# A three-stage attention front in which queries go through transposed key weights, with two banks for outputs and values and a layer norm that is split between engines

## The reference, cut to what matters

```python
# parts 0 and 2 (weights Wq 256x256, Wk and Wv 128x256, Wo 256x256)
Q = query @ Wq + bq;  K = key @ Wk + bk;  V = key @ Wv + bv
weights = softmax(Q @ K.T * 256 ** -0.5, axis=-1)
return query + (weights @ V) @ Wo + bo
# part 1: softmax over the QUERY axis, and a layer norm at the end
q = emb @ Wq + bq;  k = latent @ Wk + bk;  v = latent @ Wv + bv
w = softmax(q @ k.T / 16, axis=1)
x = w @ v + emb
return (x - mean(x)) * rsqrt(var(x) + EPS) * gamma + beta
```

## Time and profile before

| | |
|---|---|
| median of 3 runs | 2909.15 us (2907.28 to 2910.56) |
| the profiled execution, its own time | 2909.43 us |
| its span in the trace | 2907.6 us (1.83 us lie around it) |
| busy share: PE, DVE, ACT, POOL | 96%, 59%, 45%, 40% |
| the front in the span | 0 to 215.77 us |
| granted TensorE clock over the span | 0.995 |

### The profile page before, as it was taken

How to read it: one execution, slowest core, us unless ns; L and a number is a source line. 1 busy time by engine, 2 the same in 40 slices (tenths; PEclk the granted TensorE clock), 3 DMA queues, 4 the chain that set the end, 5 groups by cost and what they waited for, 6 DMA issues and landing times.

```text
span 2907.6 us, 65193 instructions
## 1 busy us (share of the span) xinstructions
PE 2792.9 (96%) x24616; PEld 2324.0 (80%) x24616; DVE 1725.4 (59%) x6432; ACT 1304.0 (45%) x4273; POOL 1173.6 (40%) x1461
## 2 busy tenths in 40 slices
PE   6878999999999999999999999999999999999999
PEld 4656888888887888888888887888888888888887
DVE  3444665665665665665665665665665655665655
ACT  2223544544544544544544544544544544544444
POOL 2213454444444444444434444434444433333333
PEclk9999999999999999999999999999999999999999
DMA  6206334335334335343335343344353344232230
GB/s 207 102 3 203 90 132 152 93 108 182 102 138 136 103 113 168 111 144 117 113 121 151 120 152 104 115 133 145 119 159 94 118 133 127 93 116 80 95 111 18
DMA packets 178766, 350.36 MB, mean 120 GB/s; under 512 B 17997, under 2 KB 142486, under 8 KB 169110
## 3 DMA queue, kind: packets, MB, share of 16 engines
q1 hardware_dynamic: 168086, 195.18, 23.3%
q0 software_dynamic: 10368, 151.00, 14.2%
HBM read 307.48 MB, written 38.67 MB: 119 GB/s over the span
## 4 chain that ended last, share of the span: by engine, by line
PE 81%; DVE 8%; POOL 6%; issue 3%; ACT 1%; DMA 0%; SPq 0%; DVEq 0%; POOLq 0%; ACTq 0%
PE proj L680 19%; PE sum L1006 16%; PE score L680 14%; PE proj L700 7%; PE sum L680 6%; PE sum L700 4%; PE proj L1027 3%; PE sum L883 3%; PE score L859 2%; POOL rstd L583 2%; PE proj L964 2%; PE tr L964 1%; PE tr L870 1%; POOL stage_parts L551 1%; PE tr L1006 1%
## 5 line engine op out<-in xcount | busy, mean ns | idle before, releaser
L634 POOL TENSOR_TENSOR prob<-prob,rtotal 128x375 f32<-128x375 f32 x672 | 543.5, 811 | 607.6 <-DVE rtotal L1622 606.5
L1081 ACT ACTIVATE prob<-prob,negmax 128x375 f32<-128x375 f32 (+1 forms) x686 | 418.0, 609 | 438.8 <-DVE negmax L1613 406.9
L1006 PE MATMUL sum<-pT,ctx 32*128 32x224 f32 (+1 forms) x4608 | 500.6, 358 | 14.9 <-DVE qcT L1605 14.9
L1006 PE MATMUL tr<-pT,ctx 32*128 32x224 f32 (+1 forms) x4608 | 500.6, 358 | 0.0
L1006 PEld LDWEIGHTS sum<-pT,ctx 32*128 32x128 f32 (+1 forms) x4608 | 417.9, 185 | 68.1 <-issue 62.6
L1613 DVE CUSTOM_DVE_ANT_0 prob<-score,cbias 128x375 f32<-128x375 f32 x672 | 356.9, 531 | 183.3 <-PE score L680 179.5
L1006 PEld LDWEIGHTS tr<-pT,ctx 32*128 32x128 f32 (+1 forms) x4608 | 417.0, 185 | 0.0
L1631 DVE STREAM_TRANSPOSE pT<-prob 128x384 f32<-128x384 f32 x672 | 372.8, 558 | 0.0
L680 PE MATMUL score<-ctx_parts,qc_high 128*128 128x376 f32 x1344 | 368.3, 355 | 0.0
L590 POOL TENSOR_TENSOR prob<-prob,rtotal 112x448 f32<-112x448 f32 x200 | 186.0, 930 | 435.0 <-DVE rtotal L1483 435.0
L1160 ACT ACTIVATE prob<-prob,negmax 112x112 f32<-112x112 f32 x800 | 298.9, 376 | 90.6 <-DVE negmax L1501 90.6
(11 more groups left out here) (243 smaller groups left out, 5315.1 us busy)
## 6 DMA issues: line engine op xcount, KB each, us to landing
w_vq_parts<-sa_v_parts POOLq DMA_DIRECT2D x24, 2048.0 KB, 8.3
w_kf_parts<-sa_k_parts POOLq DMA_DIRECT2D x24, 2048.0 KB, 8.5
w_vq_parts<-sa_q_parts POOLq DMA_DIRECT2D x24, 2048.0 KB, 9.0
w_kf<-ff_w SPq DMA_DIRECT2D x48, 1024.0 KB, 7.0
ctx<-ctx SPq DMA_DIRECT2D x192, 176.0 KB
stage<-sa_kv SPq DMA_DIRECT2D x24, 512.0 KB, 3.8
sa_v_parts<-stage_parts SPq DMA_DIRECT2D x12, 1024.0 KB, 5.2
sa_q_parts<-stage_parts SPq DMA_DIRECT2D x12, 1024.0 KB, 4.7
```

What stands on the lines that cost most here:

```text
L634: pool.tensor_tensor(row, row, rtotal[:, G * SG + i:G * SG + i + 1].broadcast_to([P, S2]), ALU.mult).then_inc(prob_ready, 1)
L1006: ins = pe.matmul(bank[:, 0:HT * R], ctx4[keys_of, m // (HALVES // NB), j, :], pT[keys_of, m % 2, :, j * R:(j + 1) * R], start=j == 0, sto ...
L1081: act.activation(o, i, ACT.Exp, bias=negmax[0:rows, col:col + 1], scale=scale, accum_out=total[0:rows, col:col + 1]).then_inc(exp_ready, 1)
```

## The change

The change touches the front only. The score Q K^T = (q Wq + bq)(c Wk + bk)^T is computed in another order: the key weights are transposed once per part (`fwkT`, two transposes through `sum1`, copied by DVE), and `front_keyed(u)` multiplies the projected query by them (2 matmuls of 224 columns into `tr0`), which gives `fqk[u]`. The scores are then products of `fqk[u]` with the raw context `ctxT`. The key bias becomes a number per query, `fbk`: in parts 0 and 2 four matmuls with a single moving column per unit, added in `front_maxima`; in part 1 two matmuls of 224 columns, and a matmul with one row of ones ahead of each score matmul. The loop is shifted so that the scores of unit u follow the keyed queries of unit u + 1. Outputs go in turn to `sum1` and `proj1` (`FRONT_OUT`), values in turn to (`proj0`, `proj1`) and (`tr0`, `tr1`) (`FRONT_VALUES`). In the layer norm DVE only does (x - mean) * rstd; gamma and beta are applied by ACT on the transposed copy (`gain`, two new loads of 128 x 2 single elements) and by POOL on the residual (a multiplication, then `add_bias`, with beta added to the bias row once). Loads are grouped anew, so that PE starts without the context and the values' weights, and the identity matrix is made first on POOL.

```diff
@@ sync
+            for n, name in enumerate(("gamma", "beta")):
+                sp.dma_start(gain[:, n, :], front[1][name].rearrange("(k p) -> p k", p=P),
+                             allow_slow_non_contiguous=True).then_inc(rows_loaded, 16)
...
@@ gpsimd
             pool.wait_ge(rows_loaded, 16 * ROW_DMAS)
+            at = Place(FRONT_LOOP)
+            pool.tensor_tensor(fbias[0:S, 1, :], fbias[0:S, 1, :], fbias[0:S, 4, :], ALU.add).then_inc(pool_step, 1)
...
             for u in range(NU):
                 inverse_std(at, 1, u)
             for u in range(NU):
-                name = FRONT_TR[u % 2]
-                before = {"proj0": 9 * NU - NU, "sum0": 2 * NU + NU}[name]
-                pool.wait_ge(ready[name], at.at(name, before + u // 2 + 1))
+                pool.wait_ge(tn_ready, at.at("tn", u + 1))
+                pool.tensor_tensor(ftw[u][:, :, :], ftn[u][:, :, :], fbias[0:S, 3, :].unsqueeze(1).broadcast_to([S, NB, E]),
+                                   ALU.mult).then_inc(pool_step, 1)
+                pool.wait_ge(pool_step, at.at("pool", at.next("pool") + 1))
                 add_bias(fbias[0:S, 1, :], ftw[u])
@@ tensor
-            pe.wait_ge(setup_done, 1)
+            pe.wait_ge(ident_ready, 1)
...
+                def front_keyed(u):
+                    for e in range(EK):
+                        pe.wait_ge(taken[f"proj{e}"], at.emptied(f"proj{e}", queried[u, e]))
...
+                    bank = fill(at, "tr0")
+                    for e in range(EK):
+                        ins = pe.matmul(bank[:, 0:T2], fwkT[:, e, :], fqT[u][:, e, :], start=e == 0, stop=e == EK - 1)
+                    if n == 1:
+                        for e in range(EK):
+                            ins = pe.matmul(bank[0:1, T2:2 * T2], fcol[:, n, 1, e:e + 1], fqT[u][:, e, :],
...
+                    else:
+                        for b in range(NB):
+                            for e in range(EK):
+                                ins = pe.matmul(bank[0:S, T2 + b:T2 + b + 1], fqT[u][:, e, b * S:(b + 1) * S],
+                                                fcol[:, n, 1, e:e + 1], start=e == 0, stop=e == EK - 1)
...
                         if n != 1:
-                            project(at, name, [fqT[u][:, e, b * S:(b + 1) * S] for e in range(EK)],
-                                    [fkT[u][:, b, e, :] for e in range(EK)])
+                            ins = pe.matmul(bank[0:S, 0:S2], query, ctxT[:, ds(first, S2)], start=True, stop=True)
...
                 front_query(0)
-                front_keys(0)
                 for u in range(NU):
                     if u + 1 < NU:
                         front_query(u + 1)
-                    front_scores(u)
-                    if u + 1 < NU:
-                        front_keys(u + 1)
+                    front_keyed(u)
+                    if u > 0:
+                        front_scores(u - 1)
+                front_scores(NU - 1)
...
@@ vector
                 def front_normalise(u):
                     wait_rstd(at)
                     for b in range(NB):
-                        ins = dve.scalar_tensor_tensor(ftn[u][:, b, :], ftw[u][:, b, :], mv2[:, u, b, 0:1], fbias[0:S, 3, :],
-                                                       ALU.subtract, ALU.mult)
-                    link(at, ins)
-                    for b in range(NB):
-                        ins = dve.scalar_tensor_tensor(ftw[u][:, b, :], ftn[u][:, b, :], rstd2[:, u, b:b + 1], fbias[0:S, 4, :],
-                                                       ALU.mult, ALU.add)
+                        ins = normalise(ftn[u][:, b, :], ftw[u], b, u)
                     ins.then_inc(tn_ready, 1)
```

More of the change, by code:

```diff
@@ L304, in attention_layers @@
         front_loaded = [sem(f"front_loaded{n}") for n in range(3)]
+        front_q_loaded = [sem(f"front_q_loaded{n}") for n in range(3)]
+        ctxT_loaded = sem("ctxT_loaded")
+        ident_ready = sem("ident_ready")
         rows_loaded = sem("rows_loaded")
@@ L464, in _ @@
             load_first(stage[:, :, :], "sa_k", "first_w_k")
-            sp.wait_ge(taken["proj1"], Place(START).emptied("proj1", 0))
+            for name in FRONT_OUT:
+                sp.wait_ge(taken[name], Place(START).emptied(name, 0))
             load_w_o(0)
@@ L1089, in front_query, with front_keyed @@
                     plus(fqT[u][:, 0, :], bank[:, 0:T2], fcol[:, n, 0, 0:1]).then_inc(taken["proj0"], 1)
-                def front_keys(u):
-                    for b in range(NB):
-                        bank = filled(at, "proj0")
-                        plus(fkT[u][:, b, 0, :], bank[:, 0:S2], fcol[:, n, 1, 0:1]).then_inc(taken["proj0"], 1)
+                def front_keyed(u):
+                    bank = filled(at, "tr0")
+                    ins = copy(fqk[u], bank[:, 0:T2])
+                    if n == 1:
+                        ins = copy(fbk[u], bank[0:1, T2:2 * T2])
+                    else:
+                        ins = copy(fbk_col[u], bank[0:S, T2:T2 + NB])
+                    ins.then_inc(taken["tr0"], 1)
                 def front_softmax(u):
@@ L1115, in _ @@
                     bank = filled(at, name)
-                    copy(ftnT[u][:, :, :].rearrange("p k t -> p (k t)"), bank[:, 0:EK * T2]).then_inc(taken[name], 1)
+                    if n != 2:
+                        copy(ftnT[u][:, :, :].rearrange("p k t -> p (k t)"), bank[:, 0:EK * T2]).then_inc(taken[name], 1)
+                    else:
+                        for k in range(EK):
+                            ins = act.activation(ftnT[u][:, k, :], bank[:, k * T2:(k + 1) * T2], ACT.Identity,
+                                                 scale=gain[:, 0, k:k + 1], bias=gain[:, 1, k:k + 1])
+                        ins.then_inc(taken[name], 1)
+                if n == 1:
+                    act.wait_ge(rows_loaded, 16 * ROW_DMAS)
+                act.wait_ge(front_q_loaded[n], 16 * FRONT_Q_DMAS)
                 front_query(0)
-                front_keys(0)
                 for u in range(NU):
@@ L1453, in _ @@
                     front_normalise(NU - 1)
-            dve.wait_ge(taken["proj1"], Place(START).emptied("proj1", 0))
+            for name in FRONT_OUT:
+                dve.wait_ge(taken[name], Place(START).emptied(name, 0))
             def parts_of_normed(at, full, high, low):
```

176 lines of the change are left out of this document (105 added, 71 removed).

## The result

The changed kernel took 2872.33 us (median of 4 runs, 2871.38 to 2873.49) against 2909.0 us for the kernel before in the same session: a ratio of 0.9873, with a 95% interval of 0.9861 to 0.9884. It is 1.3% faster, where 1.5% and 2864 us had been forecast, and it lies just above the forecast's range of 2857 to 2872 us. Three executions among the runs of the experiments were slow ones (3458, 8118 and 6934 us) and are left out of all figures. The profiled execution took 2873.49 us with a span of 2871.6 us. START begins at 179.02 us, not at 215.77 and not at the 170.8 of the forecast. That START is 8.2 us late is what the forecast missed. Behind START everything moved with it: from there to the end of the span it is 2691.8 us before and 2692.6 us after.

The account below looks back on a forecast made before the run. PE bounds most of the span, with POOL's sixth round the limit before part 2. Savings 28.5 + 12.3 - 0.7 + 1.6 + 3.3 = 45.0 from 2907.6 give 2862.6; plus 1.83 less 0.28, 2864 us; range 2857 to 2872.

Parts of the forecast that it names:

- the forecast's 7, 14 and 5: PE starts 7 us earlier; part 0's score stage shrinks by 14 us, its outputs and values by 5.
- The term of 1.0 us for the two loads of single elements: Two added loads ahead of POOL's first round delay the rounds by 1.0 us (bounds 0 and 6.4).
- 12 of 112 columns at 5.56/24 = 0.23 (2.8): Part 1's score stage: twelve 112-column matmuls a unit at 0.23 us, 2.8 of the unit's 6.0 us.
- the margin of 11 us over POOL's rounds: End of part 1: PE's last output at 106 us, POOL answers from 114.7, a margin of about 11 us.
- The first sign of being wrong: Layer norm after part 1: the forecast is wrong if POOL still waits for statistics after its sixth round.
- probabilities and clock: Bound on the forecast's sum for the probabilities and the clock: -1 to +4 us.
- this second fall of the clock: Part 2: thinner work between the probability copies, where a second clock fall would cost 3 us.
- the term as forecast: Layer norm: normalise(3) takes 2.0 us more beside POOL's new 112x512 operations (bounds 0 and 2.9).
- POOL's rounds don't bind: Rival: PE ends part 1 after the rounds, or rounds come earlier; all PE savings count, 2849 us; chance 0.05.
- The clock: Rival: after PE's idle gap the lower clock lasts through part 2's score stage, adding 16 us, 2880; chance 0.12.
- The loads: Rival: the two single-element loads hold SP or the ring over 51 us more than assumed, making it slower; chance 0.03.
- START gave nothing back: Rival of no difference: time is given back in START or the main loop to a dated transfer; chance 0.02.

Follow-up runs that it names:

- full rows: Changed kernel with part 1's bias matmuls 128 rows high (ones divided by 128) and the bias row made with 128 stationary columns: 2864.33 us, ratio 0.9845.
- The filler: Eight unread 224-column matmuls in part 2's gaps, added to the changed kernel with bias on DVE and inverse deviations ahead of POOL's sixth round: 2846.07 us.
- The run with the inverse deviation first: Changed kernel with part 1's inverse deviations moved ahead of POOL's sixth round of weights: 2872.64 us, ratio 0.9873.
- bias on DVE, inverse deviation first: Changed kernel with part 1's key bias added by DVE and its inverse deviations ahead of POOL's sixth round: 2849.29 us, ratio 0.979.

## Why the prediction was 8 us off, and what it had right

**The stages that shrink: right.** Part 1's first query starts at 60.42 us; 86.0 less the forecast's 7, 14 and 5 is 60.0. The three terms measured 6.8 (PE starts at 7.97), 13.8 and 5.9. Part 2's score stage takes 20.1 us (forecast 20.7), values 3.0 (3.8), outputs 8.0 (8.2). The last round ends at 113.2 (114.7). The term of 1.0 us for the two loads of single elements was about right: the first round's pass starts at 52.45 us, 0.9 later than the 51.54 of the kernel before. From that pass to the sixth the rounds then took 57.3 us and not 58.7; they differ by as much from run to run (without the single rows the last one ends at 114.8).

**The step that failed.** It is the term "12 of 112 columns at 5.56/24 = 0.23 (2.8)" of part 1's unit. The row that it used shows matmuls of full height; six of the twelve have one row. They cost 0.40 each, and so do their partners: 48 x 0.17 = 8.2 us more over four units. What is left of 42.7 - 24 = 18.7, some 10.5 us, is put down to the clock, which the forecast held at 1.00 because the old stage ran at 1.00. The windows agree roughly: what is missing from 1.00 in the eight windows from 72 to 103 us (five of them shown above) comes to 11.8 us. PE's last output of part 1 was ready at 125.4 and not at 106, so the margin of 11 us over POOL's rounds was eaten, PE came last, and the first query moved from the forecast's 126.2 to 132.63: 6.4 us. That POOL's rounds would bind was therefore wrong for the changed kernel. With full rows it holds: POOL doesn't wait, the first query is at 124.77, and the time is 2864.33. The first sign of being wrong, "if POOL still waits for statistics", came true (3.94 us). The list also had "if a single-column matmul costs over 0.4 us", which is the wrong operation: the single column cost 0.18, the single row 0.40.

**A term that was missing.** Part 1's unit was priced by PE alone, with no word on ACT and DVE, while part 2's had one. With full rows that shows: PE waits for ACT's exponentials, the stage takes 27.4 us and not 24, the sums behind it 12.5 and not the 7.2 of the kernel before, and the last output is ready at 113.2 and not 106. In the changed kernel PE has no such wait, as the single rows make it slower than ACT. So the single rows explain 12.2 us of PE's end (125.4 - 113.2), not all of 19.4. That full rows gave the forecast's time is in part luck: the rounds hid these 7 us, the first query came 1.4 us early, and part 2 took 1.0 us more.

**The second miss, 1.8 us,** is in "probabilities and clock". The probabilities take 8.1 us (forecast 6.5) and the sums behind them 7.2 (5.4): PE waits 1.90 and 1.22 us with short transposes between, and the sums begin at the lower level,

```profile
160.80:164.00 3.20, 3.20 (x17) 3.20 (x16) 0.89 (x3) 0.26 (x1) 0.00 (x0) 0.50 0.00 0
164.00:168.00 4.00, 4.00 (x35) 4.00 (x34) 2.98 (x5) 0.79 (x3) 0.00 (x0) 0.92 0.02 4
```

in the changed kernel. 1.6 + 1.8, less 0.6, 0.8 and 0.2 from the three stages above, is 1.8. The prediction had named this second fall of the clock, at a cost of 3, and left it out of its sum. The filler shows that it comes from the gaps and the thin work in them. The kernel before already had a row for it, in the sums of part 0, behind waits of 1.32 and 2.19 us:

```profile
60.50:67.60 7.10, 7.10 (x51) 7.10 (x50) 1.33 (x4) 1.06 (x4) 3.39 (x2) 0.75 0.22 74
```

The prediction took the 5.4 us of part 2, where the waits were 1.32, 0.29, 0.35 and 0.36 us. 6.4 + 1.8 = 8.2 is all of the lateness of START.

**The layer norm.** The single-column matmuls cost 142.52 - 141.80 = 0.72 for four, 0.18 each, and not 0.23; the trace agrees with the weight-load figure of the Trainium skill (TensorE: Matmul & The Clock Gate, "LDWEIGHTS (loading the stationary operand)"), by which the prediction had worked out 0.19. The last normalisation took 2.68 us beside POOL's new multiplication and addition, 2.0 more than its neighbour's 0.70, which is the term as forecast. The run with the inverse deviation first adds a second point: 3.52 us beside passes of 1.03 and 2.34 us (3.37 together). With no POOL operation beside it the same one took 0.74 (bias on DVE, inverse deviation first). These agree with the rule of the Trainium skill (SBUF — State Buffer, "SBUF: two separate sides") that the operation which starts first keeps the shared port pair for its whole instruction: each of DVE's two operations can wait for a whole POOL operation.

**The rivals.** "POOL's rounds don't bind" came true in its condition and not in its price: it took the late PE to be late by a little and all savings to count, while what made PE late also cost the time. The other form of it, rounds moved away, gave 2849.29 against its 2849. "The clock" came true at another place than the one named: not behind the gap ahead of part 2 (that score stage took 20.1 us), but inside a stage in which the records show no wait of PE. The loads held the rounds up by 0.9 us and not by the 51 of that rival; START gave nothing back.

**Open.** Why a matmul of one row and its full-height partner take 0.40 us is not shown. The records hint at the weight loads: with full rows the loads of a matmul begin 0.1 us ahead of it (67.10 for 67.19), with single rows together with it (69.12 for 69.12). Why the clock falls with them is not told by any record, and heights between 1 and 128 were not tried. And why runs with single rows scatter by 9 to 13 us is not settled; that the clock falls in some units and not in others goes with it.

## What to carry to other kernels

Price a matmul from a row of the same shape in all three sizes, the height of the contraction too: a bias row added by a matmul of one row may cost almost twice its columns, in the matmul behind it as well, and half of the granted clock in parts of the stage; the same matmul at 128 rows (the row repeated, divided by 128) or an addition on an engine with room is cheap. Where an independent chain stands just behind the new end of a stage, give its margin over each priced-by-analogy term, and ask what the sum is if the margin is used up: here moving the inverse deviations past one round was worth 0 or 15.6 us, depending on which side was late. When a stage on PE gets shorter, ask of the engines that free its banks how long they take, as here ACT's exponentials. When gaps with short work in them stand ahead of dense work on PE, look for a row with gaps as long: the sums of part 2 took 6.7 to 8.1 us behind waits of 1.90 and 1.22 us, and 5.4 behind one of 1.32 and three of some 0.3.

## What the runs showed of the hardware

- The granted clock fell to 0.50 in windows in which the records show PE busy for 4.00 of 4.00 us, in two different kernels, when the stage had f32 matmuls with one contraction row between others (changed kernel, 84 to 88 us; kernel before with single rows, 98 to 102 us), though not in every unit of it. With 128 rows it was 1.00 over the whole stage in the kernel before, and in the changed kernel until PE waited 2.78 us.
- f32 matmuls of 112 columns that alternate between 1 row and 128 rows start 0.40 us apart at full clock; all of 128 rows start 0.22 us apart.
- Two loads of 256 pieces of 4 bytes each took SP 0.43 and 0.47 us to issue. The first round's pass starts 0.9 us later than in the kernel before (52.45 and 51.54 us), and the last round ends at 113.2 us where the kernel before has 113.7.
